# A two-layer graph network: the deviation as two fp32r halves on TensorE, the edge pass in another order, the first mask loads in the node pass

## What is computed

```python
# layer 0, h = relu(layernorm(x))
m = concat([h[dst], h[src]]) @ W_pre.T + b_pre
mx, mn = segment_max(m, dst), segment_min(m, dst)          # 0 without an edge
mean = segment_sum(m, dst) / deg
std = sqrt(relu(segment_sum(m * m, dst) / deg - mean * mean) + EPS)
agg = concat([mx, mn, mean, std])
out = concat([h, agg, agg * log(deg + 1), agg / log(deg + 1)]) @ W_post.T + b_post
x = x + out @ W_lin.T + b_lin
# layer 1, h = relu(layernorm(x))
a = segment_sum(edge_attr, dst) / deg
x = x + relu(concat([h, a]) @ W1 + b1) @ W2 + b2
```

## Time and profile before

| | |
|---|---|
| median of 3 runs | 1456.8 us (1455.87 to 1459.47) |
| profiled execution | 1454.69 us, span 1452.9 us |
| busy over the span | PE 95%, PEld 80%, DVE 87%, ACT 78%, POOL 75% |
| node pass | to about 550 us |
| edge pass, steady | from about 620 to 1378 us |
| chain that ended last, by engine | POOL 39%, PE 37%, issue 19%, DVE 2% |

### The profile page before, as it was taken

How to read it: one execution, slowest core, us unless ns; L and a number is a source line. 1 busy time by engine, 2 the same in 40 slices (tenths; PEclk the granted TensorE clock), 3 DMA queues, 4 the chain that set the end, 5 groups by cost and what they waited for, 6 DMA issues and landing times.

```text
span 1452.9 us, 33937 instructions
## 1 busy us (share of the span) xinstructions
PE 1377.7 (95%) x8207; PEld 1155.7 (80%) x8207; DVE 1267.3 (87%) x4128; ACT 1136.8 (78%) x2760; POOL 1095.8 (75%) x1281
## 2 busy tenths in 40 slices
PE   3699999999999995999999999999999999999994
PEld 2599999999999994688888877788888877788883
DVE  4899999999999993888898888888888888888881
ACT  1699999999999993777777777777777777777772
POOL 0777777777777776678888888888888888888832
PEclk9799999999999998999999999999999999999997
DMA  2355555555555555434444444444444444444400
GB/s 83 133 204 203 206 204 203 202 202 204 203 204 202 210 184 177 134 115 123 132 118 121 119 123 120 124 124 130 140 122 125 124 124 124 125 126 129 123 23 15
DMA packets 128442, 210.96 MB, mean 145 GB/s; under 512 B 19710, under 2 KB 66041, under 8 KB 128394
## 3 DMA queue, kind: packets, MB, share of 16 engines
q1 hardware_dynamic: 106442, 162.88, 34.5%
q0 software_dynamic: 21952, 47.55, 10.8%
HBM read 123.96 MB, written 90.27 MB: 147 GB/s over the span
## 4 chain that ended last, share of the span: by engine, by line
POOL 39%; PE 37%; issue 19%; DVE 2%; DMA 1%; SPq 1%; ACT 0%; POOLq 0%; DVEq 0%
PE bank L547 13%; POOL y L456 13%; POOL rows L418 12%; POOL hs L418 10%; PE bank L556 6%; POOL pause_go L410 5%; PE bank L566 3%; PE bank L568 3%; PE bank L567 3%; PE bank L530 3%; PE bank L538 3%; DMA b_post_col<-in_L_gnn_b_post 1%; DMA table<-rows 0%; PE bank L487 0%; PE bank L588 0%
## 5 line engine op out<-in xcount | busy, mean ns | idle before, releaser
L418 POOL DMA_INDIRECT rows<-table,index x196 | 216.0, 1102 | 60.8 <-issue 60.8
L456 POOL DMA_INDIRECT y<-nout,index x196 | 208.8, 1065 | 46.5 <-issue 46.3
L581 PE MATMUL bank<-comb_lo,agg_hi 128*128 128x384 f32 x588 | 229.7, 391 | 1.4 <-ACT bank L863 1.2
L418 POOL DMA_INDIRECT hs<-table,index x196 | 191.5, 977 | 34.2 <-issue 24.8
L385 POOL TENSOR_TENSOR runs<-rows,b_all 128x512 f32<-128x512 f32 x98 | 126.0, 1286 | 112.4 <-DVE rows L1062 112.4
L547 PE MATMUL bank<-w_sb,nut 128*128 128x128 f32 x1568 | 200.7, 281 | 0.7 <-ACT nut L780 0.7
L547 PEld LDWEIGHTS bank<-w_sb,nut 128*128 128x128 f32 x1568 | 182.7, 192 | 19.0 <-issue 10.4
L585 PE MATMUL bank<-comb_hi,agg_lo 128*128 128x384 f32 x588 | 197.6, 336 | 0.1
L582 PE MATMUL bank<-comb_hi,agg_hi 128*128 128x384 f32 x588 | 197.7, 336 | 0.0
L762 ACT ACTIVATE nh<-rows,nms,nrs 128x128 f32<-128x128 f32 x392 | 161.8, 483 | 0.9 <-DVE nms L1035 0.3
L588 PE MATMUL bank<-comb_sd,agg_sd 128*128 128x384 f32 x392 | 157.9, 484 | 0.0
(11 more groups left out here) (174 smaller groups left out, 3794.2 us busy)
## 6 DMA issues: line engine op xcount, KB each, us to landing
table<-rows SPq DMA_DIRECT2D x98, 512.0 KB, 3.4
nx<-in_x SPq DMA_DIRECT2D x98, 256.0 KB, 2.8
y<-nout SPq DMA_DIRECT2D x98, 256.0 KB, 2.0
inv<-inv_row SPq DMA_DIRECT2D x49, 256.0 KB, 4.9
keepm<-keepm_row SPq DMA_DIRECT2D x49, 256.0 KB, 5.7
attr<-in_edge_attr SPq DMA_DIRECT2D x48, 256.0 KB
keep<-keep_row SPq DMA_DIRECT2D x49, 128.0 KB, 3.7
reset<-reset_row SPq DMA_DIRECT2D x49, 128.0 KB, 4.4
```

Source lines behind the costliest of these rows:

```text
L418: pool.indirect_dma_start(out=to[:, s, j, :], out_offset=None, in_=of, in_offset=bass.IndirectOffsetOnAxis(ap=column(which, c, j), axis=0) ...
L456: pool.indirect_dma_start(out=out, out_offset=bass.IndirectOffsetOnAxis(ap=column(2, c, j), axis=0), in_=eout[:, c % 2, j, :], in_offset=None,
L581: pe.matmul(acc[:, 0:SCALERS * P], hi, w_lo, start=False, stop=False, skip_group_check=True)
```

## The change

- `SD` joins the loop of `layer0`: the deviation and its folded weights are split in fp32r parts too, three products in the place of the fp32 one. ScalarE writes the deviation in place over `var`, then makes a high part; VectorE makes a low part. The set-up makes three more high and three more low weight blocks.
- TensorE, ScalarE and VectorE run their edge steps in another order.
- SP issues the attribute rows ahead of the masks' waits, and loads the masks of chunks 0 to 3 in node steps 90 to 93, ahead of those steps' other transfers.
- `square_mean` waits for both parts of the last deviation, since they read `var`.

```diff
@@ sync
+            def load_masks(c, i):
+                s = c % 4
+                m = sem(f"e_masks_in{s}")
+                for dst_sb, row in ((keep, keep_row), (reset, reset_row), (lift, lift_row), (inv, inv_row),
+                                    (keepm, keepm_row)):
+                    sp.dma_start(dst_sb[:, s, :], ...
             def node_step(k, i):
...
+                first = N_LOOP + N_LOOPS * NU
+                if first <= k < first + 4:
+                    if k == first:
+                        sp.wait_ge(r, 80)
+                    load_masks(k - first, 0)
                 c = k + 5
...
             def edge_step(k, i):
-                c = k + 4
-                if edge(c):
...                                              (masks: waits and loads)
                 c = k + 2
                 if edge(c):
...                                              (attribute rows)
+                c = k + 4
+                if edge(c) and c >= 4:
...                                              (the same five waits)
+                    load_masks(c, i)
@@ tensor, layer0
-                for a in (MX, MN, ME):
+                for a in (MX, MN, ME, SD):
...
-                if j == 0:
-                    pe.wait_ge(sem("e_std"), c + 1 + EU * i)
-                pe.matmul(acc[:, 0:SCALERS * P], agg_sd[:, c % 2, cols], comb_sd[:].rearrange("p s f -> p (s f)"),
-                          start=False, stop=True, skip_group_check=True).then_inc(sem("e_layer0"), 1)
@@ tensor, edge_step
                 if have:
-                    layer0(k, 0, i)
                     turn_attr(k, i)
                 if edge(k + 2):
                     turn_sender(k + 2, i)
+                    turn_receiver(k + 2, i)
                 if have:
+                    layer0(k, 0, i)
                     layer0(k, 1, i)
                 if edge(k + 2):
-                    turn_receiver(k + 2, i)
+                    messages(k + 2, i)
                 if behind:
                     turn_normed(k - 1, i, not edge(k + 2))
...                                              (layer0 2, hidden 0, hidden 1)
-                if edge(k + 2):
-                    messages(k + 2, i)
...                                              (layer0 3, outputs)
@@ scalar
             def deviation(c, i):
                 act.wait_ge(sem("e_var_pos"), c + 1 + EU * i)
-                if c >= 2:
-                    act.wait_ge(sem("e_layer0"), TILES * (c - 1) + TILES * EU * i)
-                act.activation(agg_sd[:, c % 2, :], var[:], ACT.Sqrt, bias=eps_col[:]).then_inc(sem("e_std"), 1)
+                act.activation(var[:], var[:], ACT.Sqrt, bias=eps_col[:]).then_inc(sem("e_std"), 1)
@@ vector, square_mean
                 if c >= 1:
-                    dve.wait_ge(sem("e_std"), c + EU * i)
+                    dve.wait_ge(sem(f"e_hi{SD}"), c + EU * i)
+                    dve.wait_ge(sem(f"e_lo{SD}"), c + EU * i)
```

More of the change, by code:

```diff
@@ L724, in _ @@
             for s, a, block_psum in comb_blocks:
-                to = comb_sd[:, s, :] if a == SD else comb_hi[:, a, s, :]
-                last = act.activation(to, block_psum, ACT.Copy)
+                last = act.activation(comb_hi[:, a, s, :], block_psum, ACT.Copy)
+                if a == SD:
+                    last = act.activation(comb_sd[:, s, :], block_psum, ACT.Copy)
             last.then_inc(sem("comb_copied"), 1)
@@ L891, in edge_step @@
                     seed(0, 0, i)
+                if ahead:
+                    scale_attr(k + 1, i)
+                if behind:
+                    squares(k - 1, i)
                 if have:
@@ L894, in edge_step @@
                 if behind:
-                    squares(k - 1, i)
                     spread(k - 1, i)
                 if edge(k + 2):
+                    receiver_turned(k + 2, i)
                     sender_turned(k + 2, i)
@@ L902, in edge_step @@
                     seed(k, 2, i)
+                if ahead:
+                    mean_squared(k + 1, i)
                 if behind:
@@ L906, in edge_step @@
                     high_part(ME, "e_mean_b", mean_b[:], k + 1, i)
-                    scale_attr(k + 1, i)
-                if edge(k + 2):
-                    receiver_turned(k + 2, i)
+                    high_part(MX, "e_max", run_max[:, (k + 1) % 2, :], k + 1, i)
+                    variance_pos(k + 1, i)
+                    high_part(MN, "e_min", run_min[:, (k + 1) % 2, :], k + 1, i)
+                    deviation(k + 1, i)
                 if behind:
                     hidden(0, 7, k - 1, i)
-                if ahead:
-                    mean_squared(k + 1, i)
                 if have:
                     seed(k, 3, i)
+                if ahead:
+                    high_part(SD, "e_std", var[:], k + 1, i)
                 if behind:
                     out_bias(k - 1, i)
+                if edge(k + 2):
+                    message_squared(k + 2, i)
+                if behind:
                     hidden(1, 1, k - 1, i)
                 if ahead:
-                    high_part(MX, "e_max", run_max[:, (k + 1) % 2, :], k + 1, i)
-                    high_part(MN, "e_min", run_min[:, (k + 1) % 2, :], k + 1, i)
-                    variance_pos(k + 1, i)
                     if k >= 0:
                         seed(k + 1, 0, i)
-                    deviation(k + 1, i)
-                if edge(k + 2):
-                    message_squared(k + 2, i)
             run_passes(act, node_step, edge_step)
@@ L1289, in edge_step @@
                 if ahead:
+                    scan_max(k + 1, i)
+                    scan_squares(k + 1, i)
                     scan_sum(k + 1, i)
@@ L1292, in edge_step @@
                     outputs(k - 2, i)
-                if ahead:
-                    scan_squares(k + 1, i)
                 if behind:
                     factors(k - 1, i)
+                if ahead:
+                    message_mean(k + 1, i)
+                if have:
+                    mix(k, 0, i)
+                if ahead:
+                    square_mean(k + 1, i)
+                    scan_min(k + 1, i)
+                    variance(k + 1, i)
+                if behind:
+                    normed_low(k - 1, i)
+                if have:
+                    mix(k, 1, i)
+                if ahead:
+                    low_part(MX, run_max[:, (k + 1) % 2, :], k + 1, i)
+                if have:
+                    scan_attr(k, i)
+                    mix(k, 2, i)
                 if edge(k + 2):
@@ L1299, in edge_step @@
                 if ahead:
-                    square_mean(k + 1, i)
-                if have:
-                    mix(k, 0, i)
-                if ahead:
-                    message_mean(k + 1, i)
-                if have:
-                    mix(k, 1, i)
-                if behind:
-                    normed_low(k - 1, i)
-                if ahead:
-                    scan_min(k + 1, i)
-                    scan_max(k + 1, i)
-                if have:
-                    mix(k, 2, i)
-                    scan_attr(k, i)
-                if ahead:
-                    variance(k + 1, i)
+                    low_part(MN, run_min[:, (k + 1) % 2, :], k + 1, i)
                     low_part(ME, mean_b[:], k + 1, i)
-                    low_part(MN, run_min[:, (k + 1) % 2, :], k + 1, i)
-                    low_part(MX, run_max[:, (k + 1) % 2, :], k + 1, i)
                 if have:
@@ L1322, in edge_step @@
                     negative_mean(k, i)
+                if ahead:
+                    low_part(SD, var[:], k + 1, i)
             run_passes(dve, node_step, edge_step, first_step=-1)
```

24 lines of the change are left out of this document (16 added, 8 removed).

## The result

| | before | after |
|---|---|---|
| median | 1456.9 us | 1484.4 us (1482.1 to 1487.0) |
| ratio | | 1.018, 95% interval 1.017 to 1.020 |
| span of the profiled execution | 1452.9 us | 1485.2 us |

The change costs 27.5 us. The forecast was 1447 us in a range of 1426 to 1482, with 0.36 on slower. The time is rival C's, just above the range. When some of the experiments ran, the kernel before itself took 1652 us (e1 to e4) or 1619 us (e12) instead of 1457, so their numbers stand only beside that.

A forecast was written before the change was run, and what follows sets the result against it. TensorE bounds the edge pass at 17.23 us a chunk, POOL some 0.15 behind. POOL becomes the bound: -1.4 - 5.1 - 4 + 1 = -9.5, 1454.7 to 1445.2; profiled run 2.1 below median, so 1447 us (1426 to 1482).

The forecast's parts named there:

- rival C: Edge pass: POOL walks and falls behind; rounds of 17.8 us give 1475 us, 18.0 gives 1484; chance 0.31.
- TensorE's part: Edge pass: three fp32r products for the fp32 one save 0.5 us a chunk; 16.7 us needed, -24 us.
- POOL's part: Edge pass: no new work, but VectorE's two-input instructions hold POOL 1.43 us a chunk; round 17.2 us, -1.4 us.
- The share of seven tenths: POOL in the edge pass before: hold of 1.3 us seen against 1.87 expected at random starts.
- The walk: POOL's 18 starts laid over VectorE's new edge step: rounds lose 1.7, 2.3, 1.3, 1.5 us; in step at 18.0.
- the lag's terms: Edge pass, POOL slower: slack -5.6, turn_sender's new place +1.8, last steps at TensorE's pace -1.3; sum -5.1 us.
- the slack of 5.6 us: Edge pass: a gather's last DMA lands at 1048.0 and is needed at 1053.6, 5.6 us later.
- The transition: Between the passes: gathers start 5 us earlier, freed of mask loads and a slow store; -4 us (-1 to -5).
- The set-up: Set-up: three more low weight blocks cost +0.6 us, with their copies +1 us.
- Rival A: Edge pass: POOL falls into step with TensorE within 16.7 us; -27 us, so 1430 us; chance 0.27.
- Rival D: Edge pass: ScalarE's seeds miss by 0.1 to 0.2 us a tile; step 17.1 to 17.3, 1448 us; chance 0.06.
- SP's part: Mask issues in node steps 90 to 93 delay stores 2.2 us: nothing, at worst +3; attribute rows matter only for scale_attr.

The follow-up runs named there:

- e1: The kernel after without the small additions ahead of POOL's indirect DMAs: 1645 us, beside 1652 for the kernel before.
- e4: The kernel after with SP's steps of the kernel before (mask loads and attribute rows): 1710 us, beside 1652 for the kernel before.
- e12: The kernel before with two more small POOL additions in each gather, eight instead of six a chunk: 1605 us, beside 1619 for the kernel before.
- e7: The kernel before without the small additions ahead of POOL's indirect DMAs, run again: 1456.3 us, ratio 1.000.
- e13: The kernel after without POOL's additions, masks of chunks 0 to 3 loaded in edge steps again, attribute rows still ahead of the masks' waits: 1432.7 us.
- e5: The kernel after without the small additions ahead of POOL's indirect DMAs, run again: 1428.0 us, 0.980 of the kernel before.
- e10: The halves alone (three fp32r products, split deviation) in the kernel before's engine order and SP steps, without POOL's additions: 1448.4 us.
- e11: The kernel after, with POOL's additions, with SP's steps of the kernel before, run again: 1657.5 us, 1.138 of the kernel before.
- e2: The kernel before without the small additions ahead of POOL's indirect DMAs: 1895 us, beside 1652 for the kernel before.
- e8: The kernel after, additions kept, with VectorE's four low parts subtracting from a PSUM tile instead of the SBUF aggregate: 1432.1 us, ratio 0.983.
- e6: The halves alone (three fp32r products, split deviation) in the kernel before's engine order and SP steps, POOL's additions kept, run again: 1450.1 us, 0.995.

## Why the prediction was wrong, point by point

- **TensorE's part** was right: 16.7 us a step forecast, 16.71 measured wherever POOL wasn't late. So was what bounds the kernel before: e7 didn't move.
- **The step that failed** is POOL's part, in the sentence "by the share seen, POOL's hold is 1.3 x 3.94/3.58 = 1.43, its round 17.2 us". The share of seven tenths belonged to the old order's phases, and I carried it over to an order in which every two-input instruction stands elsewhere. Measured: a hold of 2.2 us, where 1.43 was forecast, above the 2.0 of random starts as well; the round was 18.11. The 15.76 without holds was right (15.9).
- **The walk was the better evidence.** Laid out by hand, the new order never fell into step at 16.7 and did at 18.0; 18.11 was measured. I gave it "evidence for rival C, not a price", for fear of 0.3 us in the positions. Rival C at 18.0 stood in the text with 1484 us, and the median is 1484.4. That it fits to the tenth is luck: the step was 0.11 longer, 5 us in 46 steps, and the profiled run was 2.6 us above the median where the sum took it for 2.1 below. The range ended at 1482, between C's sums for rounds of 17.8 and 18.0.
- **The other terms of the sum.** With the measured step the sum closes: 46 x 0.88 = +40, less 5.1, less 4, plus 1, is +32, and the spans differ by 32.3. It closes as a total only. Of the lag's terms, the slack of 5.6 us was mis-sized: it took 3.65 us from the start of a gather's last DMA to its landing, from a row between the passes, and where `turn_sender` waits in the steady part of after it is 5.7 us or more (6.45 in the row below). By the distances of 8.3 and 5.0 us the slack was 3.3. The transition was sized right: 4.7 us by the medians of e13 and e5, and the 3.0 of their profiled runs has a node pass in it that began 1.85 us later in e5 for no reason in the code. But POOL's first addition ran at 553.84 us, not near 551 (before: 555.62): the node pass began late, and the masks cost it 1.3 us, which I had put at nothing. From its first matmul to the issue of the last table store but one it is 477.9 us before and in e13, and 479.2 after and in e5.

```profile
1081.43 6.45 DMA rows<-table,index
```

- **The set-up** was sized right: the twelve low blocks took 2.35 us for 1.76, the 0.6 of the sum. The node pass began 1.9 us later instead of 1, but 1.3 of that was there before the first low block, and 1.05 of it is a load at the very start that took 10.48 us for 9.43.

```profile
39.54 2.35 DVE comb_lo L1112 x12
```

- **Rival A** was the right description of the kernel without the additions, and wrong for this one. **Rival D** did not come in the new order: the step is 16.71 in e5. A chain of that kind shows in e10, in the old order.
- **SP's part** was under-read: "the attribute rows ahead of the masks' waits matter only because `scale_attr` is now first on ScalarE" is the right mechanism with no price. It is 173 us of loss avoided (e11 against after), and I expected 1484 to 1490 of e11 after writing that sentence.

## What to carry to other kernels

Where a second engine stands within a per cent of the bound, count it as a bound of the changed kernel: lay its own round over the new order of the engine that it collides with, and don't scale its old delay. If such a walk and a mean disagree, the walk has the phases in it and the mean hasn't. What an instruction costs an engine is read with the gap that it replaces: about 0.1 us here, and not the 0.35 of the instruction and its own gap. And when an instruction is moved to the head of an engine's step, look up what its input waits for on the queue that loads it.

## What the runs showed that I had not expected

- The kernel after without POOL's additions runs in **1428.0 us, 2.0% faster than the kernel before** and 3.8% faster than the one after. The same edit gives nothing in the kernel before (e7), and costs 15% where that kernel takes 1652 us (e2). Beside those 1652 us the kernel after without them took 1645 (e1), and the kernel after itself wasn't timed there. So the gain is shown only where the kernel before takes 1457 us, and why is open.
- One operand moved from SBUF to PSUM in four VectorE instructions a step is worth 52 us (e8), without any change in the length of a VectorE instruction (a low part takes 0.69 us in both).
- A POOL instruction can be held for nearly a whole scan, 1.01 us, even if it is an addition of one element per partition.
- An instruction of POOL that comes only just behind the start of a scan isn't held. In e6 25 began 0.056 to 0.064 us behind one, with 1.18 us of it left, and lasted their free length.
